# A fused decoder layer: in the last group the weighted sum of c moves to TensorE, the z products move between two halves of an expert's product, and three smaller moves

## The reference, cut to what matters

```python
s = (c @ w_c + b_c)[:, :, None] + (q @ w_q + b_q)[:, None, :] + cq     # c: 112 tokens, q: 375 context rows
a = softmax(s, axis=2)
c2q_att = einsum('bcq,bqd->bcd', a, q)
b_att = softmax(max(s, axis=2), axis=1)                                 # one weight per token
q2c_att = einsum('bc,bcd->bd', b_att, c)[:, None, :]                    # the weighted sum of c
z = concatenate([c, c2q_att, c * c2q_att, c * q2c_att], axis=-1) @ W_l.T + b_l
```

## Time and profile before

| | us |
|---|---|
| median of 3 runs | 655.91 |
| lowest and highest run | 655.82, 656.21 |
| the profiled execution, whole | 655.94 |
| its span in the profile | 654.1 |
| TensorE busy | 645.0 |
| VectorE busy | 470.1 |
| ScalarE busy | 329.7 |
| GpSimd busy | 241.3 |

### The profile page before, as it was taken

How to read it: one execution, slowest core, us unless ns; L and a number is a source line. 1 busy time by engine, 2 the same in 40 slices (tenths; PEclk the granted TensorE clock), 3 DMA queues, 4 the chain that set the end, 5 groups by cost and what they waited for, 6 DMA issues and landing times. The chain is left out here.

```text
span 654.1 us, 11891 instructions
## 1 busy us (share of the span) xinstructions
PE 645.0 (99%) x3922; PEld 551.8 (84%) x3922; DVE 470.1 (72%) x1259; ACT 329.7 (50%) x779; POOL 241.3 (37%) x305
## 2 busy tenths in 40 slices
PE   8999999999999999999999989999999999999997
PEld 5878888889788888897897878888888888888887
DVE  5788868878788788787888978676575765747433
ACT  4575675555756755556576454333533344334331
POOL 2256163353562633534644233223232232322221
PEclk9999999999999999999999999999999999999999
DMA  8534044051340440513624260403214033230300
GB/s 232 155 97 144 8 124 122 28 168 48 92 145 7 122 122 25 165 54 87 197 71 125 84 220 21 180 27 130 98 52 174 0 129 96 70 125 1 151 13 32
DMA packets 51806, 64.44 MB, mean 99 GB/s; under 512 B 3944, under 2 KB 49560, under 8 KB 50880
## 3 DMA queue, kind: packets, MB, share of 16 engines
q1 hardware_dynamic: 51776, 64.06, 31.5%
HBM read 56.60 MB, written 7.45 MB: 98 GB/s over the span
## 5 line engine op out<-in xcount | busy, mean ns | idle before, releaser
L1630 POOL TENSOR_TENSOR xt<-xt,cw_wide 128x512 f32<-128x512 f32 x55 | 72.5, 1318 | 187.2 <-ACT xt L1587 187.2
L1654 DVE TENSOR_TENSOR res<-bank,xt 128x512 f32<-128x512 f32 x62 | 42.6, 688 | 62.3 <-POOL xt L1630 58.3
L1591 ACT ACTIVATE a_hi<-res 128x512 fp32r<-128x512 f32 x42 | 26.7, 635 | 82.4 <-DVE res L1654 82.4
L75 PE MATMUL bank<-h_hi,w_lo 128*128 128x512 f32 x168 | 67.1, 400 | 0.1
L76 PE MATMUL bank<-h_lo,w_hi 128*128 128x512 f32 x168 | 65.9, 392 | 0.0
L77 PE MATMUL bank<-h_hi,w_hi 128*128 128x512 f32 x168 | 65.6, 390 | 0.0
L1025 POOL TENSOR_TENSOR wz_lo<-tmp,wz_hi 128x512 fp32r<-128x512 f32 x28 | 34.9, 1284 | 37.6 <-DVE tmp L1196 37.6
L643 PE MATMUL bank<-cw_wide,ctw 128*112 128x375 f32 x128 | 46.7, 486 | 0.4
L656 PE MATMUL bank<-ctxf,qg 125*112 125x256 f32 x192 | 46.7, 379 | 0.0
L1659 DVE TENSOR_TENSOR a_lo<-res,a_hi 128x512 fp32r<-128x512 f32 x42 | 30.0, 714 | 22.4 <-ACT a_hi L1591 22.4
L1587 ACT ACTIVATE xt<-bank 128x512 f32<-128x512 f32 x61 | 36.0, 590 | 14.6 <-PE bank L77 14.5
(11 more groups left out here) (241 smaller groups left out, 2016.1 us busy)
## 6 DMA issues: line engine op xcount, KB each, us to landing
cw_wide<-in_ctx_t SPq DMA_DIRECT2D x32, 375.0 KB
ctxf<-in_ctx SPq DMA_DIRECT2D x32, 375.0 KB
cw_wide<-cw_scratch SPq DMA_DIRECT2D x7, 1536.0 KB, 7.5
xt<-in_x SPq DMA_DIRECT2D x8, 448.0 KB, 3.9
x_scratch<-x2b SPq DMA_DIRECT2D x8, 448.0 KB, 3.2
x2n<-x_scratch SPq DMA_DIRECT2D x7, 512.0 KB, 4.6
cw_wide<-cw_scratch SPq DMA_DIRECT2D x7, 512.0 KB, 4.2
x2t<-x_scratch SPq DMA_DIRECT2D x7, 512.0 KB, 3.9
```

The costliest lines, as they stand in the source:

```text
L75: pe.matmul(dst, a_lo, b_hi, start=first, stop=False, **kw)
L1591: act.activation(a_hi[n % (AHEAD + 1)][:, :], af[(p + n) % 2][:, :], ACT.Copy).then_inc(a_hi_ok, 1)
L1630: pool.tensor_tensor(sg[b][:, :], sg[b][:, :], cw_wide[p][:, ORDER[n], :], ALU.mult).then_inc(sgw_ok, 1)
L1654: dve.tensor_tensor(af[b][:, :], u_bank[b][:, :], sg[b][:, :], ALU.mult).then_inc(af_ok, 1)
```

## The change

It does five things. (1) In the last group PE turns `mrow` into columns (one transpose) in place of the four spreading products; DVE copies them (`b_col`), and PE forms the sum of c with eight float32 products of one moving column each. DVE copies the 8 columns into `q2c`, where it had two multiplications and a reduction. (2) In the last group the gate and up product of expert 1 is parted: gate, then the four `z_c`, then up, then `turn_h3`, which stood ahead of `z_c`. (3) ACT splits two `wz` ahead of `copy_cw`, DVE makes the low part of the shared expert's activation ahead of `x2_sum`, and POOL's last multiplication waits for that in place of the last `wz_lo`. (4) At the start there are four zero products for five, and v's bias products stand behind the turns of h. (5) In the second block's first group `turn_cw` and `copy_cw` move from n = 7 to n = 8.

```diff
--- before.py
+++ after.py
@@ -367,6 +367,7 @@
             shared_f = wl_f[:, KB:2 * KB + 1, :].rearrange("p b d -> p (b d)")
             assert GU + D == (KB + 1) * D
             q2c = sb("q2c", [P, G, KB])
+            b_col = sb("b_col", [L, G])
             cb = ctw
 
             w_in = [sem(f"qkv_weights{k}_in") for k in range(KB)]
@@ -406,9 +407,10 @@
             q2c_ok, wz_ok, wz_hi_ok, wz_lo_ok = sem("q2c_ready"), sem("c_weights_ready"), sem("c_weights_hi"), sem("c_weights_lo")
             z_mm, x2_ok = sem("z_product"), sem("x2_ready")
             b_sum_ok = sem("b_sum_ready")
+            t_b, b_col_ok, q2c_mm = sem("b_att_transposed"), sem("b_att_columns"), sem("q2c_product")
 
             EARLY_LOADS, LATE_LOADS = 3, 5
-            ZERO_PRODUCTS = 5
+            ZERO_PRODUCTS = 4
             QKV_SPLITS = 2 * KB
             qkv_parts = [(slice(0, D), nwq), (slice(D, 3 * D), nw)]
             x_tiles = x.rearrange("b t d -> t b d")
@@ -534,14 +536,14 @@
                     pe.wait_ge(w_in[k], 16)
                     last = pe.matmul(m_bank[0:L, :], nb_wide[:, k, :], wqkv_f[:, k, 0:2 * D], start=(k == 0), stop=(k == KB - 1))
                 last.then_inc(bias_mm, 1)
+                pe.wait_ge(ident_ok, 16)
+                for j in range(G):
+                    turn_h(j)
                 for half in range(KB):
                     for k in range(KB):
                         last = pe.matmul(v_bank[1][:, half:half + 1], wqkv_f[:, k, 2 * D + half * P:2 * D + (half + 1) * P],
                                          nb[:, k:k + 1], start=(k == 0), stop=(k == KB - 1))
                 last.then_inc(vbias_mm, 1)
-                pe.wait_ge(ident_ok, 16)
-                for j in range(G):
-                    turn_h(j)
 
                 def z_of(j):
                     return z_bank[j // 2][0:L, (j % 2) * D:(j % 2 + 1) * D]
@@ -571,12 +573,15 @@
                                        wqkv_lo[:, k, 0:2 * D], k == 0, k == KB - 1)
                         last.then_inc(qk_mm, 1)
 
+                    def gate_up_half(n, half, w_hi, w_lo):
+                        for k in range(KB):
+                            last = mm3(pe, bank[2 * half + n][:, :], gate_up_weights(w_hi)[:, half, k, :], gate_up_weights(w_lo)[:, half, k, :],
+                                       h3_hi0[:, k, :], h3_lo0[:, k, :], k == 0, k == KB - 1)
+                        last.then_inc(gu_mm, 1)
+
                     def gate_up_early(n, w_hi, w_lo):
-                        for half, dst in enumerate((bank[n], bank[2 + n])):
-                            for k in range(KB):
-                                last = mm3(pe, dst[:, :], gate_up_weights(w_hi)[:, half, k, :], gate_up_weights(w_lo)[:, half, k, :],
-                                           h3_hi0[:, k, :], h3_lo0[:, k, :], k == 0, k == KB - 1)
-                            last.then_inc(gu_mm, 1)
+                        for half in range(2):
+                            gate_up_half(n, half, w_hi, w_lo)
 
                     def scores(j):
                         pe.wait_ge(qk_ok, ev[j])
@@ -754,13 +759,23 @@
                     turn_x(3)
                     z_c2q(1)
                     pe.wait_ge(mrow_ok, i + 1)
-                    for j in range(G):
-                        last = pe.matmul(m_bank[:, j * L:(j + 1) * L], ident[0:G, j:j + 1].to_broadcast([G, P]), mrow[:, :],
-                                         start=True, stop=True)
-                    last.then_inc(b_mm, 1)
+                    if last_group:
+                        pe.transpose(m_bank[0:L, D:D + G], mrow[:, :], ident[0:G, 0:G]).then_inc(t_b, 1)
+                    else:
+                        for j in range(G):
+                            last = pe.matmul(m_bank[:, j * L:(j + 1) * L], ident[0:G, j:j + 1].to_broadcast([G, P]), mrow[:, :],
+                                             start=True, stop=True)
+                        last.then_inc(b_mm, 1)
                     z_x3(0)
                     z_c2q(2)
                     z_x3(1)
+                    if last_group:
+                        pe.wait_ge(b_col_ok, 1)
+                        for j in range(G):
+                            for k in range(KB):
+                                n = D + G + j * KB + k
+                                last = pe.matmul(m_bank[:, n:n + 1], c[:, j, k * P:(k + 1) * P], b_col[:, j:j + 1], start=True, stop=True)
+                        last.then_inc(q2c_mm, 1)
                     if not last_group:
                         pe.wait_ge(h_lo_ok, G * (i + 1) + 2)
                         turn_h_pair(i + 1, 1)
@@ -776,12 +791,12 @@
                         turn_cw(pe, 0, h_bank[1])
                         pe.wait_ge(af_ok, 1)
                         pe.wait_ge(w01_lo_ok, 2)
-                        gate_up_early(0, wqkv_hi[:, 1, :], wqkv_lo[:, 1, :])
-                        pe.wait_ge(cwt_ok, 1)
-                        pe.wait_ge(cb_ok, i + 1)
-                        turn_h3(pe, 1)
+                        gate_up_half(0, 0, wqkv_hi[:, 1, :], wqkv_lo[:, 1, :])
                         for j in range(G):
                             z_c(i, j)
+                        gate_up_half(0, 1, wqkv_hi[:, 1, :], wqkv_lo[:, 1, :])
+                        pe.wait_ge(cwt_ok, 1)
+                        turn_h3(pe, 1)
 
                 pe.wait_ge(w_low, QKV_SPLITS)
                 group(0, False)
@@ -959,9 +974,11 @@
                         act.activation(op_hi0[:, :], af[0][:, :], ACT.Copy).then_inc(a_hi_ok, 1)
                         act.wait_ge(gu_mm, 3)
                         act.activation(sg[1][:, :], bank[1][:, :], ACT.Silu).then_inc(sg_ok, 1)
+                        wz_high(i, 0)
+                        wz_high(i, 1)
                         copy_cw(act, 0, h_bank[1])
-                        for j in range(G):
-                            wz_high(i, j)
+                        wz_high(i, 2)
+                        wz_high(i, 3)
                     else:
                         residual(i + 1)
                         h_high_pair(i + 1, 1)
@@ -1072,7 +1089,7 @@
                     if last:
                         pool.wait_ge(sg_ok, 2)
                         pool.wait_ge(cw_in, 16)
-                        pool.wait_ge(wz_lo_ok, ev[G - 1])
+                        pool.wait_ge(a_lo_ok, 1)
                         pool.tensor_tensor(sg[1][:, :], sg[1][:, :], cw_wide0[:, 0, :], ALU.mult).then_inc(sgw_ok, 1)
 
                 pool.wait_ge(consts, 4)
@@ -1343,6 +1360,9 @@
                     x3_product(1)
                     if not last:
                         h_low_pair(i + 1, 0)
+                    if last:
+                        dve.wait_ge(t_b, 1)
+                        dve.tensor_copy(b_col[:, :], m_bank[0:L, D:D + G]).then_inc(b_col_ok, 1)
                     x3_low(0)
                     x_low(2)
                     x3_product(2)
@@ -1360,13 +1380,17 @@
                         dve.wait_ge(gu_mm, 2)
                         dve.wait_ge(sg_ok, 1)
                         dve.tensor_tensor(af[0][:, :], bank[2][:, :], sg[0][:, :], ALU.mult).then_inc(af_ok, 1)
-                    dve.wait_ge(b_mm, i + 1)
-                    b_wide = m_bank[:, 0:TOK].rearrange("p (g t) -> p g t", g=G)
-                    for k in range(KB):
-                        w = dve.tensor_tensor(cb[:, :, k, :], ct[:, :, k, :], b_wide, ALU.mult)
-                    w.then_inc(cb_ok, 1)
-                    dve.wait_ge(cb_ok, i + 1)
-                    dve.reduce_sum(q2c[:, :, :], cb[:, :, :, :], AX).then_inc(q2c_ok, 1)
+                    if last:
+                        dve.wait_ge(q2c_mm, 1)
+                        dve.tensor_copy(q2c[:, :, :], m_bank[:, D + G:D + G + G * KB].rearrange("p (g k) -> p g k", g=G)).then_inc(q2c_ok, 1)
+                    else:
+                        dve.wait_ge(b_mm, i + 1)
+                        b_wide = m_bank[:, 0:TOK].rearrange("p (g t) -> p g t", g=G)
+                        for k in range(KB):
+                            w = dve.tensor_tensor(cb[:, :, k, :], ct[:, :, k, :], b_wide, ALU.mult)
+                        w.then_inc(cb_ok, 1)
+                        dve.wait_ge(cb_ok, i + 1)
+                        dve.reduce_sum(q2c[:, :, :], cb[:, :, :, :], AX).then_inc(q2c_ok, 1)
                     dve.wait_ge(q2c_ok, i + 1)
                     if not last:
                         for j in range(G):
@@ -1380,10 +1404,10 @@
                         wz_sum(3)
                         wz_low_last(2)
                         wz_low_last(3)
+                        dve.wait_ge(a_hi_ok, 1)
+                        dve.tensor_tensor(op_lo0[:, :], af[0][:, :], f32(op_hi0[:, :]), ALU.subtract).then_inc(a_lo_ok, 1)
                         x2_sum(i, 0)
                         x2_sum(i, 1)
-                        dve.wait_ge(a_hi_ok, 1)
```

(5 more changed lines are left out.)

## The result

The changed kernel takes 658.09 us (median of 10 runs, 657.63 to 658.47) against 656.20 (10 runs, 655.82 to 656.73): ratio 1.0028, 95% interval 1.0018 to 1.0038, so 1.9 us slower, clear of noise but small. Its profiled execution took 658.47, with a span of 656.7; the one before took 655.94, with 654.1. The forecast was +1.1, the right sign and 0.8 too small; the other 0.3 of its error in the absolute time is that the kernel before took 656.20 here, and 655.91 in the runs it was made from.

The account below looks back on a forecast made before the run. TensorE, busy 99% of the span, was taken as the bound, with its longest wait at the border. Border +0.68, holding the start's -0.18, and n = 8 +0.44 summed to +1.12: 657.0 against the median, range 655.8 to 658.2.

Parts of the forecast that it names:

- The start, -0.18: Start of the kernel: scores begin at 17.97 instead of 18.15, held by the projection weights' DMA; bounds 0 and -1.07.
- The sum of c on PE, +1.48 at the turn: Last group, ahead of `turn_cw`: new one-column products and type change cost +1.67, the spreading products' removal gives back -0.19.
- ACT's two high parts now ahead of `copy_cw` end just when the turn is ready, so I price that edit at nothing.: Last group, ACT: high parts end near 370.4 and cost nothing; if DVE is late, up to 0.6 each.
- The transfers, +1.30 like PE: Last group, from copy through two DMAs to POOL: this path moves with PE, 1.30 later.
- The border follows POOL: Border of the blocks: POOL ends last at 378.15, so PE restarts +0.68 later, near 378.5, after waiting some 1.1.
- The parted product works as meant: Last group's parted gate and up product: DVE's sums run under 12 passes and the turns of h.
- ends near 377.4: PE's end ahead of the border: remaining work only reordered, 1.30 behind 376.07, then some 1.1 of waiting for POOL.
- n = 8, +0.44: Second block's first group: the moved turn costs +0.44, as PE still waits for DVE's activation and loses the cover.
- whole weight loads: Rival at the 16 one-column passes ahead of the folded products: 0.188 each, 3.0 in all, result 658.4; chance 0.13.
- the border is PE's: Rival at the border: POOL is not last, PE's end sets the restart, -0.07 there, +0.44 behind, 656.3; chance 0.13.
- the clock: Rival behind the new thin products: clock falls to 1.2 GHz, 12 passes take 2.8 more, 659.8; chance 0.03.

Follow-up runs that it names:

- c4: Kernel before with DVE's low part ahead of its additions and the routing weights' turn and copy earlier, old start kept: 655.34 us, ratio 0.9993.
- a3: Changed kernel with the old start again (five zero products, v's bias ahead of the turns of h): 658.20 us, ratio to before 1.0035.
- b1: Kernel before with only the new start (four zero products, v's bias behind the turns of h): 655.90 us, ratio 0.9997.
- c1: Kernel before with DVE's low part ahead of its additions, the routing weights' turn and copy earlier, and the new start: 655.34 us, ratio 0.9992.
- b3: Changed kernel with POOL's four additions held until DVE has made its first two wz sums: 658.98 us, ratio to before 1.0047.
- b4: Changed kernel with the weighted sum of c back on DVE, the rest of the change kept: 658.16 us, ratio to before 1.0033.
- a4: Changed kernel with PE's turn of the routing weights ahead of expert 0's folded product and ACT's copy behind the first silu: 657.31 us, ratio to before 1.0019.
- c2: Kernel before with only the parted gate and up product, the sum of c still on DVE: 656.68 us, ratio 1.0013.
- a2: Changed kernel with ACT's copy of the routing weights ahead of its first two high parts again: 658.48 us, ratio to before 1.0035.
- a1: Changed kernel with the second block's turn and copy of the routing weights back at n = 7: 657.64 us, ratio to before 1.0024.
- c3: Kernel before with only the sum of c on PE, the last product whole: 657.52 us, ratio 1.0026.
- b2: Kernel before with only DVE's low part of the shared expert's activation ahead of its two sums into x: 655.50 us, ratio 0.9989.

## Why the prediction had the sign and was 0.8 short

*The start, -0.18.* The mechanism was right: the projection weights are late next, and both readings behind the term hold for the execution they were made on, 18.15 as PE's end of the q and k products and 17.97 as what the landing allows (c4 has 17.98 with the same landing). But PE came later than the landing allows in only one of the six profiles with the old start, so the term of a usual execution should have been near 0. No gain can be measured either (a3, b1, c1 against c4).

*The sum of c on PE, +1.48 at the turn.* The trace has 1.47, and that is partly luck. The passes cost 1.78 where 1.67 was written (from the product behind `mrow` to `turn_cw` it is 11.64, before 9.86): 1.70 from the first of them to the next product, and 0.08 behind it, near the 0.07 of the forecast. The way past the transpose saved 0.31 where 0.19 was written (0.76 from `mrow` to the next product in place of 1.07). Two errors of a tenth cancel. The rule of the Trainium skill on weight loads (TensorE: Matmul & The Clock Gate, section LDWEIGHTS), which the prediction set beside its 0.10, gave an estimated 1.71 for the passes, and the trace agrees with its 1.70. The new wait of 0.55 for `x3_low` was foreseen.

*"ACT's two high parts now ahead of `copy_cw` end just when the turn is ready, so I price that edit at nothing."* **This is the term that was mis-sized: 0.59.** The text gave its condition, "if DVE is late they push it by up to 0.6 each", and DVE was late: its sums now began 10.66 behind `mrow` in place of 11.64, ran beside POOL's last adds and took 0.72 more. The prediction moved DVE's sums 1.1 earlier without asking what runs there on the other engines. b3 shows it: without the adds beside them the sums take 1.68 and the copy follows its turn by 0.64, the high parts still ahead of it. b4 shows that the place of the copy costs the kernel as much with an early turn.

*The transfers, +1.30 like PE.* They took 0.19 more; from copy to POOL it is between 6.42 and 6.76 in the profiles where POOL waits for them, so a sum on one profile can't be better than some 0.3 here. Why they differ is open.

*The border follows POOL.* Right in the changed kernel, and a4 shows it, by 1.05. The wait at the border is 1.36, foreseen 1.1.

*"The parted product works as meant", and PE "ends near 377.4".* **Wrong.** From `mrow` on PE ends at 20.52, where 18.51 + 1.48 = 19.99 was to be expected, 0.53 later, and in c2 the parting costs 0.76 alone. I had checked that DVE's sums run under the first half, but not what stands behind `z_c` in place of it. In the changed kernel POOL hides this; it is why a2 and b3 gained nothing.

*n = 8, +0.44.* Right (0.45 in a1; the wait for the activation is 1.21, foreseen 1.3).

Forecast and trace so differ by 0.18 + 0.59 + 0.19 = 0.96, and 1.12 + 0.96 = 2.08 is the 2.09 of the profiled executions; against the medians it is 0.8. The measured 658.09 lies close under the range's upper end of 658.2, which had been set there for whole weight loads; these did not come, so it was room left for another cause that held the missing 0.8. Of the rivals, "whole weight loads" is out, since a pass took 0.106 on average; "the border is PE's" is out for the change but true of a2, a4, b3 and c2; the clock did not fall behind the thin products in the changed kernel's profile.

## What to carry to other kernels

Where several engines end within a microsecond of a barrier, price an edit by all of their ends: here a2, a4 and b3 each moved one end and showed the next. When work moves to another time, list what the other engines do at that time, above all VectorE and GpSimd. An order that puts a dependent product ahead of its independent cover only moves the wait; and the cheapest edit, DVE's low part moved into idle time ahead of the additions, is the only one of the four tried alone that pays: 0.4 us in the trace and 0.7 in the medians, just measurable, inside a change that costs 1.9. And a sum made on one profile takes over what was particular to that execution, as the start's 0.18 did.

## What was not expected of the hardware

The granted clock fell to half, 1.2 GHz, at the border in two of the 14 profiles, after the two longest waits there: 1.83 in b1 and 2.88 in c3. In the other profiles the wait was 1.73 or less and the clock stayed. Timeline of PE in b1:

```profile
378.09 0.31 PE L77 MATMUL bank<-shared_hi,op_hi 128*128 128x256 f32 x1
378.21 0.41 PE L75 MATMUL bank<-shared_hi,op_lo 128*128 128x256 f32 x1
378.42 0.41 PE L76 MATMUL bank<-shared_lo,op_hi 128*128 128x256 f32 x1
```

Passes are 0.21 apart in place of 0.12, until 381.40. It cost b1 nothing: the product behind the turn, for n = 8, starts at 403.69 as before, since up to there the chain runs over DVE and POOL and PE has room. In c3 half the clock for 5.73 is 2.9 of PE's work, and the same product came 26.84 behind the restart in place of 25.89, 0.95 later.

These two profiles give no threshold. With its one fall b1's profile has a mean granted clock of 0.997. The same 0.997 stands at 27 of the 72 executions of the kernel before that were run beside the experiments, at 5 of 11 of b1 and at 1 of 10 of the change, but at none of the 74 of a1 to a4, b2, c1, c2 and c4. So the kernel before seems to lose clock in about a third of its executions too, though its profile shows none; where it does is not shown. Among the 72 it makes no clear difference to the time, but the two slowest executions of b3 and the slowest of b4 (659.04) are among those with 0.997.
